# Token projection in three rounded products over two neighbouring banks, and weights' transposes that wait only for what they read

## The chip, the core and the metric

The kernel runs on one core of a Trainium2 chip. The metric is the device time of one execution in microseconds (us). Before the change three runs took 1888.12 to 1890.75, median 1889.14.

## The reference

One transformer layer on 2048 tokens of width 512: latent attention with 16 heads, then a feed-forward matrix, each with a residual and a layer norm. All is float32. The part that the change touches is the projection of the tokens at the head of the attention:

```python
cq = rms_norm(hidden_states @ w_qa.T, q_a_ln_w)          # 384 columns
ckv = hidden_states @ w_kva.T                            # 128 + 64 columns
k_pe = ckv[..., KVLR:].reshape(b, s, 1, DR).transpose(0, 2, 1, 3)
k_pe = k_pe * cos + rotate_half(k_pe) * sin
ckv_l = rms_norm(ckv[..., :KVLR], kv_a_ln_w)
```

So each token is multiplied by 576 columns of weights. `cq` later makes the queries; `ckv_l` is key and value of every head (the heads' own matrices are folded into the queries' and the output's weights by the kernel); `k_pe` is the rotary part of the keys.

## The kernel before

The program has three phases, each a block of its own in which all engines start together: preparing (lines 96 to 578), attention, and the output's feed-forward. Only the first is touched. It runs a hardware loop of four iterations `c`; each treats four tiles `t` of 128 tokens and, beside them, one group of four heads' weights.

A tile goes like this. TensorE turns its x with four transposes into bank X (`turn_x`, line 331); ScalarE copies it to `x_t` (`copy_x`, line 443). TensorE multiplies it by the turned weights `wa_t` (`project`, lines 343 and 351): a plain float32 product counts two matmul records per 128 rows, so a tile has 8 records of 512 columns into bank `PROJ` and 8 of the last 64 columns into `KP`. ScalarE takes the sums of squares of the 384 and the 128 columns (474, 476). VectorE makes the rotary part (545 to 551) and adds the epsilon (555), POOL raises to the power -1/2 (284). ScalarE scales the 384 columns to `cq_n` (482), VectorE the 128 to `c_n` (561), and makes the value tiles (567, 569). TensorE transposes the results (`turn_results`, lines 359 to 366). Then each result is stored in two rounded (fp32r) halves: `hi` on ScalarE rounds it (467, 469), `lo` on VectorE stores the remainder (530, 532); `tok_lo` counts the remainders, three a tile.

Beside tile t TensorE does some of the 14 fills of the heads' weights (`beside`: fills 0 to 2, 3 to 6, 7 to 9, 10 and 11; 12 and 13 at the end): three products of 512 columns ("nope", line 385), three pairs of transposes ("pe", 391), four times four transposes ("turn", 397) and four products ("out", 404). ScalarE and VectorE empty each by `split` as rounded value and remainder (458, 522), a "turn" by one copy (450). The fills use banks 5 to 7 in turn.

The order on every engine is that of the code. TensorE: `project(t)`, `turn_x(t+1)`, the fills beside t, `turn_results(t-1)`. ScalarE: squares, copy of the next x, splits, `cq_n(t)`, `hi(t-1)`. VectorE: rotary part, epsilon, splits, `c_n(t)`, `lo(t-1)`. After the loop the angles' tables are transposed, copied and stored to DRAM by 16 DMAs of SP; then the attention starts.

At the start SP issues the loads one after the other: identity, w_qa, w_kva, its tail, both norms' weights, mask, cos, sin, and a copy of x to DRAM; POOL issues x and the first group's weights. TensorE waits for identity, both norms and all of w_qa and w_kva, then turns them (316, 318); ScalarE copies them (436, 437).

Of the kernel before, what the change touches and what calls it, by code (L numbers as in the profile page):

```python
# [14 lines left out]
P = 128  # L15
S = 2048
HID = 512
# [21 lines left out]
def chunk(c):  # L39

    return (c + 1) % NCH
# [54 lines left out]
def prepare_phase(nc, m, x, w_qa, w_kva, w_qb, w_kvb, w_o, q_ln, kv_ln, ident_in, mask_in, cos_in, sin_in):  # L96
# [6 lines left out]
    with ExitStack() as ctx:  # L103
# [10 lines left out]
        def sb(name, n):  # L114
            return ctx.enter_context(nc.sbuf_tensor(name, [P, n], F32))[:, :]
# [8 lines left out]
        wa_t = stage(KH * WA).rearrange("p (k n) -> p k n", k=KH)  # L124
        x_in = stage(4 * HID).rearrange("p (t i) -> p t i", t=4)
        x_t = [sb(f"x_t{b}", HID) for b in range(2)]
# [18 lines left out]
        const_loaded = sem("const_loaded")  # L145
        consts_made = sem("consts_made")
        wa_loaded = sem("wa_loaded")
        wa_turned = sem("wa_turned")
        wa_copied = sem("wa_copied")
# [3 lines left out]
        xt_copied = sem("xt_copied")  # L153
# [30 lines left out]
        X, PROJ, TR = m.bank[0], m.bank[1:3], m.bank[3]  # L184
        KP, KT = m.bank[4][:, 0:DR], m.bank[4][:, P:2 * P]
# [24 lines left out]
        def fill_bank(n):  # L210
            return m.bank[5 + n % 3]

        def last_in_bank(n):

            return max(f for f in range(FILLS) if f % 3 == n % 3)
# [19 lines left out]
        def _(sp):  # L235
            sp.dma_start(m.ident[:, :], ident_in).then_inc(const_loaded, 16)
            sp.dma_start(wa_rows[:, 0:3, :], w_qa.rearrange("(o p) i -> p o i", p=P)).then_inc(wa_loaded, 16)
            sp.dma_start(wa_rows[:, 3, :], w_kva[0:C]).then_inc(wa_loaded, 16)
            sp.dma_start(wa_tail[0:DR], w_kva[C:C + DR]).then_inc(wa_loaded, 16)
            sp.dma_start(q_w, q_ln.rearrange("(k p) -> p k", p=P),  # L240
                         allow_slow_non_contiguous=True).then_inc(const_loaded, 16)
            sp.dma_start(kv_w, kv_ln.rearrange("(k p) -> p k", p=P),
                         allow_slow_non_contiguous=True).then_inc(const_loaded, 16)
# [66 lines left out]
        def _(pe):  # L310
            pe.wait_ge(const_loaded, 16 * 3)
            pe.wait_ge(wa_loaded, 48)

            for k in range(KH):
                for o in range(4):
                    pe.transpose(m.bank[k][:, o * P:o * P + P], wa_rows[:, o, k * P:k * P + P], m.ident[:, :])
            for k in range(KH):
                mm = pe.transpose(m.bank[4][:, k * DR:k * DR + DR], wa_tail[0:DR, k * P:k * P + P],
                                  m.ident[0:DR, 0:DR])
            mm.then_inc(wa_turned, 1)  # L320
            pe.wait_ge(wa_copied, KH + 1)
# [96 lines left out]
            pe.wait_ge(xt_copied, NCH * 4 + 1)  # L418
# [7 lines left out]
        def token_places(c, t):  # L426
# [3 lines left out]
            yield KT, lambda a: m.key_pe[:, a, bass.ds(chunk(c) * 512 + t * P, P)], None  # L430

        @block.scalar
        def _(act):
            act.wait_ge(wa_turned, 1)
            for k in range(KH):
                nc.scalar.copy(wa_t[:, k, 0:QLR + C], m.bank[k]).then_inc(wa_copied, 1)
            nc.scalar.copy(wa_t[:, :, QLR + C:WA], m.bank[4][:, 0:KH * DR].rearrange("p (k n) -> p k n", k=KH)
                           ).then_inc(wa_copied, 1)
            act.wait_ge(consts_made, 4)

            def copy_x(c, t):
                act.wait_ge(x_turned, 1 if c is None else c * 4 + t + 1)
                nc.scalar.copy(x_t[t % 2], X).then_inc(xt_copied, 1)

            copy_x(None, 0)
            with act.Fori(0, NCH) as c:
# [24 lines left out]
                for t in range(4):  # L471
                    b = t % 2
                    act.wait_ge(proj_ready, c * 4 + t + 1)
                    nc.scalar.activation(squares[:, 0:QLR], PROJ[b][:, 0:QLR], ACT.Square, scale=QLR ** -0.5,
                                         accum_out=means[:, 2 * b:2 * b + 1]).then_inc(squared, 1)
                    nc.scalar.activation(squares[:, QLR:QLR + C], PROJ[b][:, QLR:QLR + C], ACT.Square, scale=C ** -0.5,
                                         accum_out=means[:, 2 * b + 1:2 * b + 2]).then_inc(squared, 1)
                    copy_x(c, t + 1)
# [3 lines left out]
                    nc.scalar.activation(cq_n[b], PROJ[b][:, 0:QLR], ACT.Copy,  # L482
# [21 lines left out]
        def _(dve):  # L504
            nc.vector.memset(minus_half, -0.5).then_inc(consts_made, 1)
            dve.wait_ge(const_loaded, 16 * 3)
            nc.vector.tensor_copy(m.ident16[:, :], m.ident[:, :]).then_inc(consts_made, 1)
            dve.wait_ge(wq_free, 16)
            nc.vector.tensor_copy(m.mask16[:, :], mask).then_inc(consts_made, 1)

            nc.vector.tensor_scalar(q_w, q_w, SCALE, None, ALU.mult).then_inc(consts_made, 1)
            dve.wait_ge(consts_made, 4)
            dve.wait_ge(wo_free, 16)
            dve.wait_ge(cq_free, 16)
            nc.vector.memset(m.small[:, 60:61], 0.0).then_inc(tok_lo, TOK)
            nc.vector.memset(m.small[:, 61:62], 0.0).then_inc(split_lo, SPLITS)
            with dve.Fori(0, NCH) as c:
# [17 lines left out]
                for t in range(4):  # L535
# [4 lines left out]
                    kp = KP.rearrange("p (a d) -> p a d", a=2)  # L540
# [20 lines left out]
                    nc.vector.tensor_scalar(c_n[b], PROJ[b][:, QLR:QLR + C], rstd[:, 2 * b + 1:2 * b + 2],  # L561
# [1188 lines left out]
```

## Time and profile before

| what | us |
|---|---|
| median of three runs | 1889.14 |
| profiled execution | 1888.2 |
| its span (first to last instruction) | 1886.5 |
| before the loop | 0 to 24.3 |
| four iterations | 24.3 to 156.3 |
| table copies and stores | to 176.4 |
| attention and feed-forward | from 176.4 |

Over the span TensorE (PE) is busy 91%, VectorE (DVE) 74%, ScalarE (ACT) 58%, GpSimd (POOL) 52%. In the views PE is a matmul or transpose, PEld the load of its stationary operand. A line of a timeline joins neighbouring instructions of one kind (x8 is eight), with the start of the first; the duration of the last runs on while the next instruction begins, so the pace of matmuls is read from one start to the next. A bracket says how long the engine was idle before it and what ended that. PEclk is the granted clock of TensorE, 1.00 for 2.4 GHz and 0.50 for 1.2 GHz.

### The profile page before, as it was taken

What the parts mean: (1) busy time and instruction counts of PE and PEld (TensorE: products, weight loads), DVE (VectorE), ACT (ScalarE), POOL (GpSimd) and SP (SyncE); (2) the same over time, 40 slices, a digit from 0 to 9 for tenths busy, and PEclk for the clock granted to TensorE, in tenths of its full rate; (3) what the DMA queues carried; (4) which work ended last, traced back from release to release, by engine and by line L of the source; (5) the groups of instructions that cost most, each with busy time, mean ns of one, the idle gap of its engine ahead of it and who ended that gap; (6) DMA issues with size and microseconds to landing.
All of it is one profiled execution on the core that took longest, in us unless ns stands there. A gap on an engine that the chain in (4) does not pass through costs nothing. (4 is left out here: it accounts for less than half of the span.)

```text
span 1886.5 us, 28030 instructions
## 1 busy us (share of the span) xinstructions
PE 1725.7 (91%) x8729; PEld 1396.3 (74%) x8729; DVE 1393.6 (74%) x2503; ACT 1096.9 (58%) x2092; POOL 971.9 (52%) x883
## 2 busy tenths in 40 slices
PE   5995699999999999999988899999999999998586
PEld 4564578888888888888877688888887887886442
DVE  1552368888888888878766588888888888888366
ACT  2553256666676666657545566666666766666220
POOL 2320135555555555556543455565555665556455
PEclk9997899999999999999989899999999999999889
DMA  7876212121211311112121221212112111100321
GB/s 231 305 304 211 64 49 62 46 68 40 92 50 57 98 60 52 61 51 84 57 67 34 94 75 36 67 39 96 49 53 101 42 48 35 52 31 31 123 73 56
DMA packets 90138, 152.99 MB, mean 81 GB/s; under 512 B 17872, under 2 KB 60368, under 8 KB 87632
## 3 DMA queue, kind: packets, MB, share of 16 engines
q1 hardware_dynamic: 81168, 103.60, 17.5%
q0 software_dynamic: 7104, 23.60, 3.8%
q10 hardware_dynamic: 1728, 24.12, 3.0%
q8 instruction: 67, 1.10, 0.2%
q14 instruction: 71, 0.58, 0.1%
HBM read 87.30 MB, written 51.38 MB: 74 GB/s over the span
## 5 line engine op out<-in xcount | busy, mean ns | idle before, releaser
L1320 POOL TENSOR_TENSOR split_p<-pool,split_p 128x512 fp32r<-128x512 f32 x544 | 702.9, 1294 | 542.3 <-ACT split_p L1265 541.9
L1143 PE MATMUL rows<-q_c,key_c 128*128 128x512 f32 x1632 | 478.9, 402 | 27.9 <-issue 15.9
L1253 ACT COPY pool<-rows 128x512 f32<-128x512 f32 x480 | 281.8, 587 | 266.7 <-PE rows L1143 264.7
L1397 DVE TENSOR_TENSOR top<-rows,top 128x512 f32<-128x512 f32 x420 | 289.0, 688 | 146.6 <-ACT pool L1253 143.5
L1412 DVE TENSOR_TENSOR pool<-bank,pool 128x512 f32<-128x512 f32 x544 | 370.1, 680 | 27.0 <-PE bank L1161 27.0
L1258 ACT ACTIVATE pool<-pool 128x512 f32<-128x512 f32 x544 | 345.9, 636 | 18.8 <-DVE pool L1412 18.3
L1265 ACT CAST split_p<-pool 128x512 fp32r<-128x512 f32 x544 | 333.2, 612 | 25.0 <-PE bank L1174 25.0
L1143 PEld LDWEIGHTS rows<-q_c,key_c 128*128 128x128 f32 x1632 | 290.4, 190 | 76.2 <-issue 27.1
L1143 PE MATMUL rows<-q_pe,key_pe 128*128 128x512 f32 x1088 | 339.1, 393 | 0.0
L1424 DVE TENSOR_TENSOR bank<-bank,pool 128x512 f32<-128x512 f32 x480 | 331.1, 690 | 0.1
L1143 PEld LDWEIGHTS rows<-q_pe,key_pe 128*128 128x128 f32 x1088 | 205.7, 189 | 45.6
L1171 PE MATMUL bank<-split_p,val 128*128 128x512 f32 x544 | 215.1, 395 | 9.2 <-ACT o_sum L1271 9.0
L1174 PE MATMUL bank<-split_p,val 128*128 128x512 f32 x544 | 214.8, 395 | 5.2 <-POOL split_p L1320 4.9
L1172 PE MATMUL bank<-split_p,val 128*128 128x512 f32 x544 | 213.2, 392 | 0.0
L1203 PE MATMUL rows<-wo,o_t 128*128 128x512 f32 x528 | 136.2, 408 | 22.9 <-POOL o_t L1325 18.3
L1203 PEld LDWEIGHTS rows<-wo,o_t 128*128 128x128 f32 x528 | 101.1, 196 | 55.7 <-issue 34.3
L1325 POOL TENSOR_TENSOR o_t<-o_sum,o_t 128x512 fp32r<-128x512 f32 x64 | 82.4, 1287 | 94.9 <-ACT o_t L1283 94.7
L1171 PEld LDWEIGHTS bank<-split_p,val 128*128 128x128 f32 x544 | 102.5, 188 | 34.8 <-ACT o_sum L1271 11.7
L1174 PEld LDWEIGHTS bank<-split_p,val 128*128 128x128 f32 x544 | 102.7, 189 | 33.2 <-POOL split_p L1320 11.5
L1172 PEld LDWEIGHTS bank<-split_p,val 128*128 128x128 f32 x544 | 102.7, 189 | 21.3
L1283 ACT CAST o_t<-o_sum 128x512 fp32r<-128x512 f32 x64 | 39.7, 620 | 126.2 <-DVE o_sum L1436 99.0
L1109 PE MATMUL rows<-cq,wq 128*128 128x256 f32 x792 | 105.0, 287 | 0.0
(159 smaller groups left out, 2058.8 us busy)
## 6 DMA issues: line engine op xcount, KB each, us to landing
cq<-cq_dram SPq DMA_DIRECT2D x28, 768.0 KB, 5.0
y<-y_dram SPq DMA_DIRECT2D x64, 256.0 KB, 3.0
y_dram<-y SPq DMA_DIRECT2D x64, 256.0 KB, 2.0
wq_dram<-wq ACTq DMA_DIRECT2D x4, 2304.0 KB, 11.5
wo_dram<-wo ACTq DMA_DIRECT2D x4, 2048.0 KB, 10.6
q_pe<-by_sin SPq DMA_DIRECT2D x256, 32.0 KB, 1.8
q_pe<-by_cos SPq DMA_DIRECT2D x256, 32.0 KB, 1.8
table<-table_dram SPq DMA_DIRECT2D x31, 256.0 KB, 2.9
```

What stands on the lines that cost most here:

```text
L1143: mm = pe.matmul(by_head(out), k, q, start=(z == 0), stop=(z == 4))
L1171: pe.matmul(OUT, m.val[:, 0, j, :], split_p[:, n % 2, 0, :], start=(t == 0), stop=False)
L1172: pe.matmul(OUT, m.val[:, 1, j, :], split_p[:, n % 2, 0, :], start=False, stop=False)
L1174: pe.matmul(OUT, m.val[:, 0, j, :], split_p[:, n % 2, 1, :], start=False, stop=(t == keys(it) - 1)).then_inc(values_done, 1)
L1203: mm = pe.matmul(aux(u), o_t[:, a, h * P:h * P + P], m.wo[:, b, h, :], start=(n == 0), stop=(n == 3 * HG - 1))
L1253: nc.scalar.copy(slot(n), SCORES[n % N_SCORES]).then_inc(scores_copied, 1)
L1258: nc.scalar.activation(slot(n), slot(n), ACT.Exp).then_inc(exp_done, 1)
L1265: nc.scalar.copy(split_p[:, n % 2, 0, :], slot(n)).then_inc(p_hi, 1)
L1320: nc.gpsimd.tensor_tensor(split_p[:, n % 2, 1, :], slot(n), stored(split_p[:, n % 2, 0, :]), ALU.subtract).then_inc(p_lo, 1)
L1397: nc.vector.tensor_tensor(out, SCORES[n % N_SCORES], slot(number(it, 0)) if t == 1 else out, ALU.max).then_inc(scores_maxed, 1)
L1412: nc.vector.tensor_tensor(slot(n), MAXES, slot(n), ALU.add).then_inc(shifted, 1)
L1424: nc.vector.tensor_tensor(TOTAL, TOTAL, slot(n), ALU.add).then_inc(summed, 1)
```

## The change

- x and the turned weights are each kept as a rounded value and a rounded remainder (`x_hi`, `x_lo`, `wa_hi`, `wa_lo`). ScalarE's copy makes the first, a new subtraction on VectorE the second (`rest_of_x`, one per tile, and five for the weights). The projection is hi by hi, hi by lo and lo by hi: 3 x 4 stationary operands, each against two halves of 288 columns, 24 matmuls a tile.
- The 576 columns lie across the border of two neighbouring banks, in bank pairs 0, 1 and 2, 3 by turns. The turned rotary part of tile t lies in the same pair as its products. x is turned in bank 4, results in bank 5, and fills have banks 6 and 7.
- `project(t)` waits for the remainders (`tok_lo`) of the tile two before ahead of its first matmul.
- ScalarE copies the next x before the squares, and waits for the rotary parts ahead of the squares.
- Weights' transposes wait for the identity and w_qa and w_kva alone, and the tail's for the tail. w_kva is loaded ahead of w_qa. The angles come in quarters, the first iteration's ahead of the norms' weights, the others behind the mask; they are waited for in the loop. VectorE's first memset of `tok_lo`, which the first projection now waits for, stands behind the mask, the norms' weights and the first quarter.

```diff
-        X, PROJ, TR = m.bank[0], m.bank[1:3], m.bank[3]
-        KP, KT = m.bank[4][:, 0:DR], m.bank[4][:, P:2 * P]
+        X, TR, PART = m.bank[4], m.bank[5], WA // 2
+
+        def projected(t):
+
+            return m.rows[:, 1024 * (t % 2) + 512 - PART:1024 * (t % 2) + 512 + PART]
+
+        def turned_rotary(t):
+
+            return m.rows[:, 1024 * (t % 2) + 1024 - P:1024 * (t % 2) + 1024]
...
         def fill_bank(n):
-            return m.bank[5 + n % 3]
+            return m.bank[6 + n % 2]
...
-            sp.dma_start(m.ident[:, :], ident_in).then_inc(const_loaded, 16)
+            def load_angles(c):
+                for table, source in ((cos, cos_in), (sin, sin_in)):
+                    sp.dma_start(table[:, 4 * chunk(c):4 * chunk(c) + 4, :],
+                                 source.rearrange("(t p) d -> p t d", p=P)[:, 4 * chunk(c):4 * chunk(c) + 4, :]
+                                 ).then_inc(angles_loaded[c > 0], 16)
+
+            sp.dma_start(m.ident[:, :], ident_in).then_inc(ident_loaded, 16)
+            sp.dma_start(wa_rows[:, 3, :], w_kva[0:C]).then_inc(wa_loaded, 16)
             sp.dma_start(wa_rows[:, 0:3, :], w_qa.rearrange("(o p) i -> p o i", p=P)).then_inc(wa_loaded, 16)
-            sp.dma_start(wa_rows[:, 3, :], w_kva[0:C]).then_inc(wa_loaded, 16)
-            sp.dma_start(wa_tail[0:DR], w_kva[C:C + DR]).then_inc(wa_loaded, 16)
+            sp.dma_start(wa_tail[0:DR], w_kva[C:C + DR]).then_inc(tail_loaded, 16)
+            load_angles(0)
...
             sp.dma_start(mask, mask_in).then_inc(wq_free, 16)
-            sp.dma_start(cos, cos_in.rearrange("(t p) d -> p t d", p=P)).then_inc(wo_free, 16)
-            sp.dma_start(sin, sin_in.rearrange("(t p) d -> p t d", p=P)).then_inc(cq_free, 16)
+            for c in range(1, NCH):
+                load_angles(c)
 
...
-            pe.wait_ge(const_loaded, 16 * 3)
-            pe.wait_ge(wa_loaded, 48)
+            pe.wait_ge(ident_loaded, 16)
+            pe.wait_ge(wa_loaded, 32)
 
             for k in range(KH):
                 for o in range(4):
-                    pe.transpose(m.bank[k][:, o * P:o * P + P], wa_rows[:, o, k * P:k * P + P], m.ident[:, :])
+                    mm = pe.transpose(m.bank[k][:, o * P:o * P + P], wa_rows[:, o, k * P:k * P + P], m.ident[:, :])
+                mm.then_inc(wa_turned, 1)
+            pe.wait_ge(tail_loaded, 16)
             for k in range(KH):
-                mm = pe.transpose(m.bank[4][:, k * DR:k * DR + DR], wa_tail[0:DR, k * P:k * P + P],
+                mm = pe.transpose(TR[:, k * DR:k * DR + DR], wa_tail[0:DR, k * P:k * P + P],
                                   m.ident[0:DR, 0:DR])
             mm.then_inc(wa_turned, 1)
-            pe.wait_ge(wa_copied, KH + 1)
...
-                    pe.wait_ge(xt_copied, c * 4 + t)
+                    pe.wait_ge(x_rest, c * 4 + t)
...
             turn_x(None, 0)
+            pe.wait_ge(wa_rest, 1)
             with pe.Fori(0, NCH) as c:
 
                 def project(t):
-                    pe.wait_ge(xt_copied, c * 4 + t + 1)
+                    pe.wait_ge(x_rounded, c * 4 + t + 1)
                     if t >= 2:
 
-                        pe.wait_ge(cn_done, c * 4 + t - 1)
-                    for k in range(KH):
-                        pe.matmul(PROJ[t % 2], x_t[t % 2][:, k * P:k * P + P], wa_t[:, k, 0:QLR + C],
-                                  start=(k == 0), stop=(k == KH - 1))
-
-
-                    if t:
-                        pe.wait_ge(rope_parts, c * 12 + 3 * t)
-                    pe.wait_ge(tok_lo, TOK + c * TOK + 3 * max(t - 1, 0))
-                    for k in range(KH):
-                        mm = pe.matmul(KP, x_t[t % 2][:, k * P:k * P + P], wa_t[:, k, QLR + C:WA],
-                                       start=(k == 0), stop=(k == KH - 1))
+                        pe.wait_ge(tok_lo, TOK + c * TOK + 3 * (t - 1))
+                    else:
+                        pe.wait_ge(tok_lo, c * TOK + 3 * (t + 3))
+                    terms = [(x_hi, wa_hi, k) for k in range(KH)] + [(x_hi, wa_lo, k) for k in range(KH)] \
+                        + [(x_lo, wa_hi, k) for k in range(KH)]
+                    for n, (xs, ws, k) in enumerate(terms):
+                        if n == 2 * KH:
+                            pe.wait_ge(x_rest, c * 4 + t + 1)
+                        for at in (0, PART):
+                            mm = pe.matmul(projected(t)[:, at:at + PART], xs[t % 2][:, k * P:k * P + P],
+                                           ws[:, k, at:at + PART], start=(n == 0), stop=(n == 3 * KH - 1))
                     mm.then_inc(proj_ready, 1)
 
...
                     pe.wait_ge(krot_done, c * 8 + 2 * t + 2)
-                    if t < 3:
-
-                        pe.wait_ge(rope_parts, c * 12 + 3 * t + 6)
-                    pe.transpose(KT, k_rot[t % 2], m.ident[:, :]).then_inc(turned, 1)
+                    pe.transpose(turned_rotary(t), k_rot[t % 2], m.ident[:, :]).then_inc(turned, 1)
...
-                    if n < 3:
+                    if n < 2:
                         pe.wait_ge(split_lo, c * SPLITS + split_of[last_in_bank(n)] + 1)
                     else:
-                        if fills[n - 3][0] == "turn":
-                            pe.wait_ge(wot_copied, c * HG + fills[n - 3][1] + 1)
+                        if fills[n - 2][0] == "turn":
+                            pe.wait_ge(wot_copied, c * HG + fills[n - 2][1] + 1)
                         else:
-                            pe.wait_ge(split_lo, SPLITS + c * SPLITS + split_of[n - 3] + 1)
+                            pe.wait_ge(split_lo, SPLITS + c * SPLITS + split_of[n - 2] + 1)
...
-            act.wait_ge(wa_turned, 1)
...
+                act.wait_ge(wa_turned, k + 1)
+                nc.scalar.copy(wa_hi[:, k, 0:QLR + C], m.bank[k]).then_inc(wa_rounded, 1)
...
             copy_x(None, 0)
+            act.wait_ge(consts_made, 4)
...
                     act.wait_ge(proj_ready, c * 4 + t + 1)
-                    nc.scalar.activation(squares[:, 0:QLR], PROJ[b][:, 0:QLR], ACT.Square, scale=QLR ** -0.5,
+                    copy_x(c, t + 1)
+                    act.wait_ge(rope_parts, c * 12 + 3 * t + 3)
+                    nc.scalar.activation(squares[:, 0:QLR], projected(b)[:, 0:QLR], ACT.Square, scale=QLR ** -0.5,
                                          accum_out=means[:, 2 * b:2 * b + 1]).then_inc(squared, 1)
-                    nc.scalar.activation(squares[:, QLR:QLR + C], PROJ[b][:, QLR:QLR + C], ACT.Square, scale=C ** -0.5,
+                    nc.scalar.activation(squares[:, QLR:QLR + C], projected(b)[:, QLR:QLR + C], ACT.Square, scale=C ** -0.5,
                                          accum_out=means[:, 2 * b + 1:2 * b + 2]).then_inc(squared, 1)
-                    copy_x(c, t + 1)
                     for n in beside[t]:
...
+            def rest_of_x(c, t):
+                dve.wait_ge(x_rounded, 1 if c is None else c * 4 + t + 1)
+                nc.vector.tensor_tensor(x_lo[t % 2], X, stored(x_hi[t % 2]), ALU.subtract).then_inc(x_rest, 1)
+
...
-            dve.wait_ge(const_loaded, 16 * 3)
+            dve.wait_ge(ident_loaded, 16)
             nc.vector.tensor_copy(m.ident16[:, :], m.ident[:, :]).then_inc(consts_made, 1)
+            for k in range(KH):
+                dve.wait_ge(wa_rounded, k + 1)
+                nc.vector.tensor_tensor(wa_lo[:, k, 0:QLR + C], m.bank[k], stored(wa_hi[:, k, 0:QLR + C]), ALU.subtract)
+            dve.wait_ge(wa_rounded, KH + 1)
+            nc.vector.tensor_tensor(wa_lo[:, :, QLR + C:WA], wa_tails(), stored(wa_hi[:, :, QLR + C:WA]), ALU.subtract
+                                    ).then_inc(wa_rest, 1)
+            rest_of_x(None, 0)
             dve.wait_ge(wq_free, 16)
             nc.vector.tensor_copy(m.mask16[:, :], mask).then_inc(consts_made, 1)
 
+            dve.wait_ge(wo_free, 16)
+            dve.wait_ge(cq_free, 16)
             nc.vector.tensor_scalar(q_w, q_w, SCALE, None, ALU.mult).then_inc(consts_made, 1)
             dve.wait_ge(consts_made, 4)
-            dve.wait_ge(wo_free, 16)
-            dve.wait_ge(cq_free, 16)
+            dve.wait_ge(angles_loaded[0], 32)
             nc.vector.memset(m.small[:, 60:61], 0.0).then_inc(tok_lo, TOK)
             nc.vector.memset(m.small[:, 61:62], 0.0).then_inc(split_lo, SPLITS)
...
-                    kp = KP.rearrange("p (a d) -> p a d", a=2)
+                    if t == 3:
+                        dve.wait_ge(angles_loaded[1], 32 * (NCH - 1))
+                    kp = projected(t)[:, QLR + C:WA].rearrange("p (a d) -> p a d", a=2)
...
+                    rest_of_x(c, t + 1)
...
```

The copy of the weights on ScalarE goes bank by bank, each followed by VectorE's subtraction.

## Rows read from the trace of the kernel before

**Rows 1.** Second iteration: us, busy of PE, PEld, DVE, ACT, POOL, PEclk, DMA share.

```profile
58.48:91.09 32.61, 30.11 (x156) 19.76 (x155) 16.84 (x59) 18.29 (x50) 10.33 (x17) 1.00 0.79 301
```

**Rows 2.** Timeline of TensorE in that iteration: start, us, engine, line, operation, idle before.

```profile
58.48 3.69 PE L343 MATMUL rows<-pool,x_t 128*128 128x512 f32 x8
...
63.29 2.84 PE L385 MATMUL bank<-pool 128*128 128x128 f32 x24
65.97 3.60 PE L343 MATMUL rows<-pool,x_t 128*128 128x512 f32 x8
...
70.24 0.61 PE L331 MATMUL rows<-ident,pool 128*128 128x128 f32 x4
...
72.71 0.66 PE L397 MATMUL bank<-ident,pool 128*128 128x128 f32 x4 [1.20 <-DVE wq L522]
...
73.75 3.60 PE L343 MATMUL rows<-pool,x_t 128*128 128x512 f32 x8
...
90.49 0.55 PE L359 MATMUL rows<-ident,cq_n 128*128 128x128 f32 x3 [1.30 <-DVE key_pe L530]
```

**Rows 3.** Timeline of ScalarE and VectorE, the iteration's second tile.

```profile
70.44 0.49 ACT L474 ACTIVATE squares<-rows 128x384 f32<-128x384 f32 x1 [3.11 <-PE bank L351]
...
71.17 0.59 ACT L443 COPY x_t<-rows 128x512 f32<-128x512 f32 x1
...
73.89 0.59 ACT L482 ACTIVATE cq_n<-rows,small 128x384 f32<-128x384 f32 x1
...
74.50 0.35 DVE L561 TENSOR_SCALAR c_n<-rows,small 128x128 f32<-128x128 f32 x1 [1.07 <-ACT cq_n L482]
...
76.30 0.28 DVE L530 TENSOR_TENSOR key_pe<-bank,key_pe 128x128 f32 x1
```

**Rows 4.** Timeline of TensorE in the attention: rounded (fp32r) matmuls at full clock.

```profile
183.11 2.32 PE L1109 MATMUL bank<-cq,wq 128*128 128x256 f32 x18
185.27 1.00 PE L1122 MATMUL rows<-cq,wq 128*128 128x256 f32 x7
...
205.97 0.86 PE L1143 MATMUL rows<-q_c,key_c 128*128 128x512 f32 x3
206.67 0.63 PE L1143 MATMUL rows<-q_pe,key_pe 128*128 128x512 f32 x2
```

**Rows 5.** Groups of instructions by line, the span's first 180 us: busy us, mean ns.

```profile
L522 DVE SCALAR_TENSOR_TENSOR wq<-bank,small,wq 128x512 fp32r<-128x512 f32 x12 | 9.0, 751 | 5.1 <-ACT wq L458 4.2
...
L458 ACT ACTIVATE wq<-bank,small 128x512 fp32r<-128x512 f32 x12 | 8.2, 687 | 1.7 <-PE bank L385 0.8
...
L522 DVE SCALAR_TENSOR_TENSOR wq<-bank,small,wq 128x256 fp32r<-128x256 f32 x12 | 5.1, 478 | 2.7 <-ACT wq L458 2.7
...
L458 ACT ACTIVATE wq<-bank,small 128x256 fp32r<-128x256 f32 x12 | 4.9, 498 | 0.0
```

**Rows 6.** Line 1369, attention: ns min/median/max, first and last start us.

```profile
L1369 DVE TENSOR_TENSOR q_c<-bank,q_c x20: 682/691/693, 186.1 to 1703.9; 128x512 fp32r<-128x512 f32 x20
```

**Rows 7.** Timeline of TensorE at the loop's start and in the attention, and one stage.

```profile
24.30 5.13 PE L343 MATMUL rows<-pool,x_t 128*128 128x512 f32 x8 [0.74 <-ACT x_t L443]
...
1039.72 0.50 PE L1171 MATMUL bank<-split_p,val 128*128 128x512 f32 x1 [2.77 <-ACT o_sum L1271]
...
1041.10:1044.50 3.40, 3.40 (x10) 2.63 (x9) 3.27 (x6) 2.87 (x6) 3.40 (x4) 0.52 0.00 0
```

**Rows 8.** Timeline of the start, and a DMA issue (KB, us from issue to landing).

```profile
1.78 0.49 SPq L238 DMA_DIRECT2D wa_rows<-in_L_attn_w_kva  x1
...
16.19 3.67 PE L316 MATMUL rows<-ident,wa_rows 128*128 128x128 f32 x16 [16.19 <-DMA small<-in_L_attn_kv_a_ln_w]
...
17.64 0.23 DVE L509 CAST mask<-pool 128x128 bf16<-128x128 f32 x1 [1.25 <-DMA pool<-const_mask]
...
22.26 0.06 DVE L515 MEMSET small<- 128x1 f32 x1 [4.31 <-DMA sin<-const_sin]
...
wa_rows<-in_L_attn_w_kva SPq DMA_DIRECT2D x1, 256.0 KB, 7.0
```

More of the change, by code:

```diff
@@ L112, in stage, with sb @@
             return m.pool[:, at - n:at]
-        def sb(name, n):
-            return ctx.enter_context(nc.sbuf_tensor(name, [P, n], F32))[:, :]
+        def sb(name, n, dt=F32):
+            return ctx.enter_context(nc.sbuf_tensor(name, [P, n], dt))[:, :]
         WA = QLR + C + DR
@@ L123, in prepare_phase @@
         mask = stage(P)
-        wa_t = stage(KH * WA).rearrange("p (k n) -> p k n", k=KH)
         x_in = stage(4 * HID).rearrange("p (t i) -> p t i", t=4)
-        x_t = [sb(f"x_t{b}", HID) for b in range(2)]
+        wa_hi = sb("wa_hi", KH * WA, F32R).rearrange("p (k n) -> p k n", k=KH)
+        wa_lo = sb("wa_lo", KH * WA, F32R).rearrange("p (k n) -> p k n", k=KH)
+        x_hi = [sb(f"x_hi{b}", HID, F32R) for b in range(2)]
+        x_lo = [sb(f"x_lo{b}", HID, F32R) for b in range(2)]
         cq_n = [sb(f"cq_n{b}", QLR) for b in range(2)]
@@ L143, in prepare_phase @@
         rstd = m.small[:, 16:20]
-        const_loaded = sem("const_loaded")
+        ident_loaded = sem("ident_loaded")
+        angles_loaded = [sem(f"angles_loaded{n}") for n in range(2)]
         consts_made = sem("consts_made")
         wa_loaded = sem("wa_loaded")
+        tail_loaded = sem("tail_loaded")
         wa_turned = sem("wa_turned")
-        wa_copied = sem("wa_copied")
+        wa_rounded = sem("wa_rounded")
+        wa_rest = sem("wa_rest")
         x_loaded = [sem(f"x_loaded{t}") for t in range(4)]
         x_turned = sem("x_turned")
-        xt_copied = sem("xt_copied")
+        x_rounded = sem("x_rounded")
+        x_rest = sem("x_rest")
         proj_ready = sem("proj_ready")
@@ L180, in prepare_phase, with wa_tails @@
         wo_free, cq_free = m.wo_free, m.cq_free
-        X, PROJ, TR = m.bank[0], m.bank[1:3], m.bank[3]
-        KP, KT = m.bank[4][:, 0:DR], m.bank[4][:, P:2 * P]
+        X, TR, PART = m.bank[4], m.bank[5], WA // 2
[3 more added lines that the diff above has]
+            return m.rows[:, 1024 * (t % 2) + 1024 - P:1024 * (t % 2) + 1024]
+        def wa_tails():
+            return TR[:, 0:KH * DR].rearrange("p (k n) -> p k n", k=KH)
         fills = [("nope", k) for k in range(KR)] + [("pe", k) for k in range(KR)] \
@@ L210, in fill_bank @@
         def fill_bank(n):
-            return m.bank[5 + n % 3]
+            return m.bank[6 + n % 2]
         def last_in_bank(n):
-            return max(f for f in range(FILLS) if f % 3 == n % 3)
+            return max(f for f in range(FILLS) if f % 2 == n % 2)
         def split_places(n):
@@ L235, in _ @@
         def _(sp):
[L236 removed]
+            def load_angles(c):
[5 more added lines that the diff above has]
+            sp.dma_start(wa_rows[:, 3, :], w_kva[0:C]).then_inc(wa_loaded, 16)
             sp.dma_start(wa_rows[:, 0:3, :], w_qa.rearrange("(o p) i -> p o i", p=P)).then_inc(wa_loaded, 16)
[L238 to L239 removed]
+            sp.dma_start(wa_tail[0:DR], w_kva[C:C + DR]).then_inc(tail_loaded, 16)
+            load_angles(0)
             sp.dma_start(q_w, q_ln.rearrange("(k p) -> p k", p=P),
[L241 removed]
+                         allow_slow_non_contiguous=True).then_inc(wo_free, 16)
             sp.dma_start(kv_w, kv_ln.rearrange("(k p) -> p k", p=P),
[L243 removed]
+                         allow_slow_non_contiguous=True).then_inc(cq_free, 16)
             sp.dma_start(mask, mask_in).then_inc(wq_free, 16)
[L245 to L246 removed]
+            for c in range(1, NCH):
+                load_angles(c)
             sp.dma_start(m.y_dram.rearrange("t p d -> (t p) d"), x).then_inc(m.y_stored, 16)
@@ L417, in _ @@
             pe.wait_ge(split_lo, SPLITS * (NCH + 1))
-            pe.wait_ge(xt_copied, NCH * 4 + 1)
+            pe.wait_ge(x_rest, NCH * 4 + 1)
             for w, source in enumerate((cos, sin)):
@@ L429, in token_places @@
             yield TR[:, QLR:QLR + C], lambda a: m.key_c[:, a, bass.ds(chunk(c) * 512 + t * P, P)], kv_w
-            yield KT, lambda a: m.key_pe[:, a, bass.ds(chunk(c) * 512 + t * P, P)], None
+            yield turned_rotary(t), lambda a: m.key_pe[:, a, bass.ds(chunk(c) * 512 + t * P, P)], None
         @block.scalar
         def _(act):
-            act.wait_ge(wa_turned, 1)
             for k in range(KH):
[L436 to L439, printed above, removed]
+                act.wait_ge(wa_turned, k + 1)
+                nc.scalar.copy(wa_hi[:, k, 0:QLR + C], m.bank[k]).then_inc(wa_rounded, 1)
+            act.wait_ge(wa_turned, KH + 1)
+            nc.scalar.copy(wa_hi[:, :, QLR + C:WA], wa_tails()).then_inc(wa_rounded, 1)
             def copy_x(c, t):
                 act.wait_ge(x_turned, 1 if c is None else c * 4 + t + 1)
-                nc.scalar.copy(x_t[t % 2], X).then_inc(xt_copied, 1)
+                nc.scalar.copy(x_hi[t % 2], X).then_inc(x_rounded, 1)
             copy_x(None, 0)
+            act.wait_ge(consts_made, 4)
             with act.Fori(0, NCH) as c:
@@ L481, in _ @@
                     act.wait_ge(rstd_done, c * 4 + t + 1)
-                    nc.scalar.activation(cq_n[b], PROJ[b][:, 0:QLR], ACT.Copy,
+                    nc.scalar.activation(cq_n[b], projected(b)[:, 0:QLR], ACT.Copy,
                                          scale=rstd[:, 2 * b:2 * b + 1]).then_inc(cqn_done, 1)
@@ L560, in _ @@
                     dve.wait_ge(cqn_done, c * 4 + t + 1)
-                    nc.vector.tensor_scalar(c_n[b], PROJ[b][:, QLR:QLR + C], rstd[:, 2 * b + 1:2 * b + 2],
+                    nc.vector.tensor_scalar(c_n[b], projected(b)[:, QLR:QLR + C], rstd[:, 2 * b + 1:2 * b + 2],
                                             None, ALU.mult).then_inc(cn_done, 1)
```

## The prediction

> **What bounds the kernel now.** I read the stages first: one of the four iterations of the preparing loop takes 32.61 us, TensorE works in 30.11 of them at clock 1.00 [rows 1]. The reader is to see that this stage, unlike the attention behind it, is one that the diff touches, and that TensorE has 2.5 us of idle time in an iteration. Next, TensorE's timeline of that iteration [rows 2]: a tile's projection starts at 65.97 and the transposes of the next x at 70.24, so it takes 4.27 us. The idle time lies in two places, 1.20 us ahead of line 397 and 1.30 us ahead of line 359, and both end with a remainder of VectorE. Last, ScalarE's and VectorE's timeline of the same tile [rows 3]: the last remainder of tile 0's results (`lo(0)`, line 530, key_pe) ends at 76.30 + 0.28 = 76.58, which is 2.83 us after the projection of tile 2 began (73.75). That lateness costs little today, since only the 64-column product waits for it, behind 3.4 us of the 512-column one.
>
> **The projection.** Removed: 16 matmuls a tile in 4.27 us. Added: 24 rounded ones of 288 columns. The nearest rows are the rounded matmuls of the attention [rows 4]: 18 of 256 columns from 183.11 to 185.27, 0.120 us each; three of 512 from 205.97 to 206.67, 0.233 each. On the line between them 288 columns are 0.134, and 24 are 3.20 us. The ends are 2.88 and 5.6; I take 3.20 because 288 is near 256. Saved: 1.07 us a tile, 17 us in all, if TensorE alone set the pace. The Trainium skill ("TensorE: Matmul & The Clock Gate", "Back-to-back issue gap") gives a sustained spacing of about 131 ns at 512 columns, by which this projection would be an estimated 2.4 us (a rival, below); the trace shows 233 ns there [rows 4], so this case does not bear it out.
>
> **The new wait.** `project(t)` for t = 2 and 3 now waits for `lo(t-2)` ahead of its first matmul, because rotary transposes and products share banks. `lo(t-2)` stands on VectorE behind `c_n(t-1)`, that behind ScalarE's `cq_n(t-1)`, and that behind the projection of t-1. So projections 1, 2, 3 and the end of the iteration become one chain through three engines. I walk one iteration from the start of projection 0, with the intervals of rows 2, 3, 5 and 6. ScalarE starts 0.20 us after TensorE's last matmul (70.24 to 70.44) [rows 2, 3]; squares take 0.73 (to 71.17), `cq_n` to `c_n` 0.61, `c_n` to the end of `lo` 2.08 (74.50 to 76.58) [rows 3]. A 512-wide eviction is 0.69 on ScalarE and 0.75 on VectorE, a 256-wide one 0.50 and 0.48 [rows 5]. The new rounding's remainder of x on VectorE is like line 1369, 0.69 [rows 6]; it lies beside ScalarE's squares and sets nothing. The same holds for ScalarE's new wait for the rotary parts, done by 3.96 us where the copy of x ends at 4.44.
> - Step 0: projection to 3.20, x turned at 3.65, copied from 3.85, squares 4.33 to 5.06, first eviction 5.75, its remainder 6.55. Two fill banks instead of three let the third fill start only then (6.6, not 5.44); with 0.89 for it (24 matmuls, three fills, from 63.29 to 65.97 [rows 2]) tile 1 starts at 7.5. Before: 7.49. The third bank's loss eats the whole gain.
> - Step 1: projection to 10.7, x turned at 11.15, two small fills to 11.6. The third and fourth wait for remainders in their banks, 13.7 and 14.1; transposed results of tile 0 end at 15.1. ScalarE: squares 11.85, evictions, the copy of fill 6 at 14.7, `cq_n` 15.2; VectorE `c_n` 15.8, `lo(0)` done 17.9. Projection 2 starts at 17.95, after 2.9 us of idle TensorE. Step: 10.45 us, against 7.78 [rows 2].
> - Step 2: projection to 21.15, x turned at 21.6, the third turned fill waits for its bank (23.7), last copy 24.3, `cq_n` 24.8, `c_n` 25.4, `lo(1)` 27.5. Projection 3 at 27.55, again after 2.9 us of idling.
> - Step 3: projection to 30.75, two output fills to 32.9, `cq_n` 33.85, `c_n` 34.7, `lo(2)` 36.8, results of tile 3 turned in 0.55 to 0.60 [rows 2]: 37.4.
>
> So an iteration is 37.4 us, not 32.61: +4.8, four times +19.2. Today `lo(0)` ends 10.61 us after projection 1 began [rows 2, 3], 0.2 more than my walk has; with as much in three steps, and as much again for hand-overs I overlooked, 1.2 us an iteration is the upper bound, +5. The lower is 24 matmuls at 0.120, 0.32 us in each of four steps, -5.
>
> **The clock.** TensorE will be idle about 2.1 and 2.9 us around a few transposes in step 1, and 1.2 and 2.9 in step 2; today's loop has nothing over 1.3. In the attention an idle of 2.77 us was followed by a stretch at 0.52 [rows 7]. Eight 512-column matmuls took 5.13 us at the start, where the clock had fallen, and 3.60 later [rows 2, 7]: 1.53 a fall. Ends: no fall, and eight (two an iteration) of 1.7. I take eight of 1.3, since some of a slow stretch lies in idle time: +10.4. The fall at the first projection stays as it is.
>
> **The start.** Weights' transposes began at 16.19 on the landing of kv_ln, though w_kva, the last that most of them read, landed at 1.78 + 7.0 = 8.8 [rows 8]. All of their work, with 4 copies, 4 remainders (0.6 and 0.7 apiece) and x's first rounding, fits between 9 and 15. But projection 0 now also waits for VectorE's memset behind mask, both norms and the first quarter of the angles. Today that memset is at 22.26, behind the whole tables [rows 8], and projection 0 at 24.30, behind the transposes [rows 7]. SP issues the small loads later (two quarter tables ahead of them, 1024 packets of 128 B), with 3072 packets of the other quarters moved behind; POOL's weight loads run beside them as now, and one x load is issued as soon as the first x is turned. Mask today lands at 17.6, sin at 22.2 [rows 8]. Between these, and 1 us on either side, 18.5 to 23 for the memset: I take projection 0 at 21.5, -2.8. Moved behind as well are the copy of x to y, and the six other quarters that SP issues. Tile 3 alone waits for those quarters, some 25 us later, and the copy is read only in the attention. Where the cover of the early weights goes, nothing is lost: they end 6 us ahead of need.
>
> **Sum** against the profiled execution's own 1888.2 us (its span is 1886.5; 0.9 under the median 1889.14 of the runs): -2.8 + 19.2 + 10.4 = +26.8, **1915 us**. Attention and the feed-forward behind it start as soon as the stage ends and are unchanged, the table's stores after the loop included.
>
> **Rivals.**
> - The same wait, clock unhurt: 1888.2 - 2.8 + 19.2 = 1904.6. For it: 1.3 us of idling does nothing today, and transposes break the gaps. Against it: [rows 7].
> - Faster: TensorE's work sets the loop and the remainders come in time. The place is the wait at projections 2 and 3; it decides if `lo(0)` ends before tile 0's results are turned, so 2.8 us sooner than now. Then each of 16 tiles saves 1.07 and the start 2.8: 1868. Against it stands 76.58 over 73.75 [rows 2, 3], and that each link of the chain follows from the one before.
> - Products of 288 columns cost like 512 ones: 24 x 0.233 = 5.6 us, +2.4 on each of 16 tiles on top of the forecast, 1953. Rows at 256 speak against it.
> - Products cheaper than any row here, at 0.100 us apiece: 0.8 less on each of 16 tiles, 1902. No row goes below 0.120 for 256 columns [rows 4]. This is where the Trainium skill's spacing ("TensorE: Matmul & The Clock Gate", "Back-to-back issue gap") would put it.
> - The change does not remove the start's wait (other loads land late as well): +2.8, 1918. The order of the queue speaks against it; it is inside the range.
> - The clock stays low for most of the stage: an iteration's four projections, 12.8 us on the chain, double, +51 in all on the unhurt clock's time: 1956.
>
> **How the numbers follow.** Forecast 0.60 (the late start within it), unhurt clock 0.23, cheaper products 0.03, low clock or dear products together 0.06, faster 0.04, and 0.04 that start and walk are so far off that they cancel. The range goes from the unhurt clock less the cheaper matmuls (1900) to eight full falls and today's latencies (some 1925, with 1 for the start): 1900 to 1926. A measurement of this kernel tells about 0.2% (3.8 us) from nothing. Faster 0.04, same 0.04, slower 0.92.
>
> **What would show it.** Right: an iteration of 37 to 41 us; PE's first matmul of projections 2 and 3 idle about 2.9 us until DVE key_pe; fill 2 waiting for a remainder of wq; clock under 1.00 inside the loop; projections of 3.2 us at full clock; projection 0 near 21.5. Wrong: idle under 1 us ahead of projections 2 and 3, an iteration under 33, or rounded matmuls off 0.134 by more than 0.02.

## The result, and the profile after

The changed kernel took 1925.75 us (median of four runs, 1923.99 to 1926.6), the kernel before 1889.95 beside it: a ratio of 1.0182, 95% interval 1.0166 to 1.0197. It is slower by 36 us. I had said 1915, in a range of 1900 to 1926; the direction and the place were right, the size was 10 us short, and the time lies only 0.25 us under the range's upper end.

The four steps of the second iteration, from the start of one tile's projection to the next (stages view of the changed kernel: length, then busy us of PE, PEld, DVE, ACT, POOL, then the granted clock, DMA share, GB/s):

```profile
66.50:74.08 7.58, 6.58 (x54) 6.39 (x53) 4.61 (x13) 3.39 (x10) 1.82 (x4) 1.00 1.04 414
74.08:84.70 10.62, 5.89 (x46) 5.22 (x44) 6.32 (x20) 5.56 (x15) 2.00 (x3) 0.88 0.58 222
84.70:96.33 11.63, 7.87 (x45) 7.40 (x45) 3.44 (x13) 4.16 (x12) 3.94 (x7) 0.79 0.16 31
96.33:107.79 11.46, 10.18 (x46) 7.40 (x47) 5.65 (x17) 5.13 (x13) 2.52 (x4) 0.87 0.92 361
```

The sum is 41.29 us, against 32.61 in [rows 1]. The reader is to see two things: the first step is as long as before (7.58 against 7.49), and the clock, 1.00 in every iteration before but the first, is 0.79 to 0.88 in the other three steps. TensorE's timeline of the same iteration shows why:

```profile
66.50 1.32 PE L376 MATMUL rows<-wa_hi,x_hi 128*128 128x288 f32 x8
...
69.78 0.60 PE L356 MATMUL bank<-ident,pool 128*128 128x128 f32 x4
70.22 1.95 PE L407 MATMUL bank<-pool 128*128 128x128 f32 x16
73.16 1.16 PE L407 MATMUL bank<-pool 128*128 128x128 f32 x8 [0.99 <-DVE wq L557]
74.08 1.30 PE L376 MATMUL rows<-wa_hi,x_hi 128*128 128x288 f32 x8
...
77.34 0.60 PE L356 MATMUL bank<-ident,pool 128*128 128x128 f32 x4
...
80.24 0.44 PE L413 MATMUL bank<-ident,pool 128*128 128x128 f32 x2 [1.87 <-DVE wq L557]
...
84.70 2.29 PE L376 MATMUL rows<-wa_hi,x_hi 128*128 128x288 f32 x8 [2.86 <-DVE key_pe L565]
...
89.90 0.60 PE L356 MATMUL bank<-ident,pool 128*128 128x128 f32 x4
...
96.33 2.29 PE L376 MATMUL rows<-wa_hi,x_hi 128*128 128x288 f32 x8 [2.74 <-DVE key_pe L565]
...
100.91 0.60 PE L356 MATMUL bank<-ident,pool 128*128 128x128 f32 x4
...
107.79 1.31 PE L376 MATMUL rows<-wa_hi,x_hi 128*128 128x288 f32 x8
```

A projection at full clock takes 74.08 to 77.34, 3.26 us for 24 matmuls. Ahead of projections 2 and 3 TensorE stands idle 2.86 and 2.74 us until the last remainder of the tile two before, and these two projections then take 5.20 and 4.58 us. VectorE's side of the first of these waits, from the same kernel's timeline, answers to [rows 3]:

```profile
82.43 0.35 DVE L599 TENSOR_SCALAR c_n<-rows,small 128x128 f32<-128x128 f32 x1 [0.72 <-ACT cq_n L505]
...
84.37 0.28 DVE L565 TENSOR_TENSOR key_pe<-rows,key_pe 128x128 f32 x1
```

`lo(0)` ends at 84.65 (84.37 + 0.28), 10.57 us after projection 1 began; before it was 10.61. The chain has kept its length, and the projection that once ran beside its last part now runs behind it.

The start, from the timeline of all engines, answers to [rows 8]:

```profile
6.03 4.05 SPq L266 DMA_DIRECT2D small<-in_L_attn_kv_a_ln_w  x1
...
8.55 3.65 PE L340 MATMUL rows<-ident,wa_rows 128*128 128x128 f32 x16 [8.55 <-DMA wa_rows<-in_L_attn_w_qa]
...
10.12 0.86 SPq L268 DMA_DIRECT2D pool<-const_mask  x1
...
21.69 0.23 DVE L543 CAST mask<-pool 128x128 bf16<-128x128 f32 x1 [6.48 <-DMA pool<-const_mask]
...
22.11 0.06 DVE L550 MEMSET small<- 128x1 f32 x1
...
22.23 2.29 PE L376 MATMUL rows<-wa_hi,x_hi 128*128 128x288 f32 x8 [8.37 <-DVE small L550]
```

The weights' transposes start 7.6 us earlier, and TensorE then waits 8.37 us for the memset, which stands behind the mask's cast. The mask was issued at 10.12 (4.13 before) and landed at 21.6. The first projection is 2.07 us earlier than before.

Where the 38.4 us between the two spans lie: -2.1 at the start, +38.3 in the loop (22.23 to 192.49, 170.26 us, against 132.0), -0.2 in the tables, and +2.4 in the attention and the feed-forward, whose code is the same.

### The profile page after: what moved, and what is told of

Read it like the earlier page. It is cut to its first block and busy times, and to the rows that moved or that the text cites. A ratio compares the mean times of both kernels' runs of the same rounds, so it can differ in the third digit from the quotient of the medians.

```text
span 1924.9 us, 28312 instructions
## 1 busy us (share of the span) xinstructions
PE 1733.2 (90%) x8857; PEld 1430.5 (74%) x8857; DVE 1408.8 (73%) x2525; ACT 1097.6 (57%) x2092; POOL 972.8 (51%) x883
```

## The experiments

### The wait alone, in the kernel before

```diff
                         pe.wait_ge(cn_done, c * 4 + t - 1)
+                        pe.wait_ge(tok_lo, TOK + c * TOK + 3 * (t - 1))
                     for k in range(KH):
                         pe.matmul(PROJ[t % 2], x_t[t % 2][:, k * P:k * P + P], wa_t[:, k, 0:QLR + C],
```

> The kernel before with one wait more: the projections of tiles 2 and 3 wait for the remainders of the tile two before ahead of their first matmul. If that wait and the clock behind it are the loss, TensorE stands idle 2.8 us ahead of projection 2 and 3.3 ahead of projection 3 in each iteration (+22 us in four, some 2 given back by the product that waited before), and a fallen clock adds 1.5 to 2 us to each of these eight projections: +32 to +38, some 1920 to 1927. If the loss lies in the rounded products, their remainders or the banks, this costs nothing of note: within 3 us of before.

Measured: 1939.22 us against 1894.19 of the kernel before on that chip, a ratio of 1.0234 (1.0208 to 1.0259): +45. One iteration and its two waits, in the stages view and TensorE's timeline of this kernel:

```profile
70.72:115.06 44.34, 35.92 (x157) 21.92 (x155) 16.87 (x59) 18.22 (x50) 10.37 (x17) 0.85 0.61 224
```

```profile
88.88 6.02 PE L344 MATMUL rows<-pool,x_t 128*128 128x512 f32 x8 [2.73 <-DVE key_pe L531]
94.74 1.00 PE L352 MATMUL bank<-pool,x_t 128*128 128x64 f32 x8
...
101.22 6.67 PE L344 MATMUL rows<-pool,x_t 128*128 128x512 f32 x8 [3.18 <-DVE key_pe L531]
107.73 1.00 PE L352 MATMUL bank<-pool,x_t 128*128 128x64 f32 x8
```

With no rounded product, no second remainder and three fill banks, an iteration is 11.7 us longer than 32.61: 5.9 of idling and 5.5 in which the two 512-column products take 5.86 and 6.51 us (88.88 to 94.74, 101.22 to 107.73) in place of 3.43. This wait makes such a loss by itself, and more than the +32 to +38 that I expected: I had priced a fall of the clock at 1.5 to 2 us a projection, and it is 2.4 and 3.1. Over the eight projections 2 and 3 of the profile it is 23.7 us of idling and 21.5 of slower products, together the 45.

### TensorE kept busy while it waits

```diff
                     if t >= 2:
+                        pe.wait_ge(x_rest, c * 4 + t + 1)
+                        for _ in range(12):
+                            pe.matmul(X, wa_hi[:, 0, 0:P], wa_hi[:, 0, 0:512], start=True, stop=True)
                         pe.wait_ge(tok_lo, TOK + c * TOK + 3 * (t - 1))
```

> The changed kernel with 12 idle matmuls of 512 columns (about 2.8 us at full clock) into the bank of the turned x, while projections 2 and 3 wait. They compute nothing that is used. If the slow projections are a matter of the clock, the 15.4 us by which projections 2 and 3 exceed 3.27 us vanish and the iteration falls to 38 us: some 1910 to 1913. If they are slow for another reason (two engines reading beside them, operands), the projections keep 4.6 to 5.9 us and the time stays at 1926 or rises by the overhang of the idle matmuls.

Measured: 1910.80 us against 1894.19, a ratio of 1.0089 (1.0071 to 1.0107). The changed kernel itself, run later on one chip with the kernel before, had 1925.27 against 1892.18, 1.0177 (1.0160 to 1.0194). Its expectation:

> The changed kernel unaltered, on the chip of the runs beside it: +36 to +37 us over before, as in the first measurement.

It was 33 over there, a little under the 36 expected. So the added work takes the loss from 33 to 36 us down to 17 (13 to 20 by the interval), within the 1910 to 1913 expected. The four steps again, in the stages view of the kernel kept busy:

```profile
62.82:70.40 7.58, 6.59 (x54) 6.40 (x53) 4.61 (x13) 3.38 (x10) 1.82 (x4) 1.00 1.03 386
70.40:81.02 10.62, 8.66 (x59) 7.37 (x57) 6.33 (x20) 5.55 (x15) 2.00 (x3) 1.00 0.68 264
81.02:90.73 9.71, 8.69 (x57) 7.62 (x57) 3.43 (x13) 4.15 (x12) 3.95 (x7) 1.00 0.20 31
90.73:100.74 10.01, 8.82 (x48) 6.11 (x47) 5.49 (x17) 5.12 (x13) 2.48 (x4) 1.00 1.01 402
```

The clock is 1.00, and the sum is 37.92. All projections of the kernel behind the first take 3.2 to 3.3 us; in the last iteration the clock still fell once, ahead of the added matmuls, which took 4.4 us in place of 3.0. My walk had said 7.5, 10.45, 9.6 and 9.85. This is the walk's own case, the wait without the clock, and it parts the loss: the projections were slow for the clock, not for their operands or for what ran beside them, since both are the same here.

### Two fill banks, in the kernel before

```diff
         def fill_bank(n):
-            return m.bank[5 + n % 3]
+            return m.bank[5 + n % 2]
```

(and `n - 3`, `n < 3` and `n % 3` in the waits likewise)

> The kernel before with two fill banks instead of three and nothing else. If the third bank's loss is a cost of its own, fills 2, 6, 9 and 12 wait 0.3 to 0.7 us each: up to 1.7 us an iteration, +4 to +7. If the waits for remainders at the end of each tile hide it, within 2 us of before.

Measured: 1901.91 against 1894.19, 1.0038 (1.0023 to 1.0052). The expectation's upper end was +7; it is +7.7 between the medians, so I had it a little too cheap. TensorE's timeline shows the waits:

```profile
61.04 3.69 PE L343 MATMUL rows<-pool,x_t 128*128 128x512 f32 x8
...
68.56 1.16 PE L385 MATMUL bank<-pool 128*128 128x128 f32 x8 [0.75 <-DVE wq L522]
...
76.30 0.44 PE L391 MATMUL bank<-ident,pool 128*128 128x128 f32 x2 [1.43 <-DVE wq L522]
...
84.06 0.66 PE L397 MATMUL bank<-ident,pool 128*128 128x128 f32 x4 [0.58 <-ACT pool L450]
...
95.86 3.68 PE L343 MATMUL rows<-pool,x_t 128*128 128x512 f32 x8
```

An iteration is 34.82 us, 2.2 more than with three banks, where I had allowed 1.7. So the third bank is worth over half of what the cheaper products can save (1.0 us on each of four tiles).

### The wait moved behind a projection

```diff
         def turned_rotary(t):
-            return m.rows[:, 1024 * (t % 2) + 1024 - P:1024 * (t % 2) + 1024]
+            return X[:, 0:P]
...
                     pe.wait_ge(x_rest, c * 4 + t)
+                    pe.wait_ge(tok_lo, TOK + c * TOK + 3 * max(t - 2, 0))
...
                     if t >= 2:
-                        pe.wait_ge(tok_lo, TOK + c * TOK + 3 * (t - 1))
-                    else:
-                        pe.wait_ge(tok_lo, c * TOK + 3 * (t + 3))
+                        pe.wait_ge(cn_done, c * 4 + t - 1)
...
                     pe.wait_ge(krot_done, c * 8 + 2 * t + 2)
+                    pe.wait_ge(x_rest, c * 4 + min(t + 3, 5))
```

> The changed kernel with the turned rotary part in the bank of the turned x, so that projections wait only for their own products to be read, and the wait for the remainders stands ahead of the next turning of x, behind a projection. If the early wait was the loss, iterations fall to 31 to 32 us with the clock at 1.00, and the start gains some 5 us: 1878 to 1884. If the three products, the new remainders or the two fill banks cost the time, iterations stay over 36 and the time over 1900.

Measured: 1884.14 against 1894.19, 0.9950 (0.9933 to 0.9966). All of the change but the place of one 128-column transpose, and the waits that go with it, is in here, and it is 10 us faster than before instead of 36 slower (1884.14 is just over the expected 1878 to 1884). The second iteration in the stages view, and its waits in TensorE's timeline:

```profile
51.93:83.77 31.84, 26.77 (x188) 23.19 (x187) 19.89 (x63) 18.31 (x50) 10.27 (x17) 1.00 0.82 313
```

```profile
58.59 1.16 PE L407 MATMUL bank<-pool 128*128 128x128 f32 x8 [0.99 <-DVE wq L557]
...
65.67 0.44 PE L413 MATMUL bank<-ident,pool 128*128 128x128 f32 x2 [1.86 <-DVE wq L557]
...
72.79 0.66 PE L419 MATMUL bank<-ident,pool 128*128 128x128 f32 x4 [1.02 <-ACT pool L472]
...
83.07 0.55 PE L383 MATMUL bank<-ident,cq_n 128*128 128x128 f32 x3 [0.68 <-DVE key_pe L565]
```

TensorE works 3.3 us less in this iteration than before, but waits 5.1 instead of 2.5, mostly for the two fill banks. The clock is 1.00 here, but not to the end. In the third iteration the same wait of 1.86 us is followed by slow transposes and a slow first part of projection 2:

```profile
97.50 0.44 PE L413 MATMUL bank<-ident,pool 128*128 128x128 f32 x2 [1.86 <-DVE wq L557]
...
99.56 2.20 PE L375 MATMUL rows<-wa_hi,x_hi 128*128 128x288 f32 x8
101.59 1.23 PE L375 MATMUL rows<-wa_lo,x_hi 128*128 128x288 f32 x8
```

That iteration takes 33.41 us (83.77 to 117.18) at a mean clock of 0.95, and in the fourth projection 2 takes 4.80. Where the gain lies is told by two starts of projection 1 in the first iteration, before and here:

```profile
33.23 3.60 PE L343 MATMUL rows<-pool,x_t 128*128 128x512 f32 x8
```

```profile
27.46 1.30 PE L375 MATMUL rows<-wa_hi,x_hi 128*128 128x288 f32 x8
```

It is 5.8 us earlier here, because projection 0 no longer waits for the memset, and the attention's first instruction is 6.0 us earlier (170.43 against 176.38). So in the profile the whole gain is made at the start, and the rest of the loop, from projection 1 on, is as long as before: what the cheaper products save, some 0.8 us an iteration, two falls of the clock take back.

### The start alone, in the kernel before

The loads, semaphores and waits of the changed kernel as in its diff; projection, banks and engines' orders of before.

> The kernel before with the changed loads and the changed waits of the weights' transposes alone. In the changed kernel the start gained 2.1 us, because projection 0 waited for VectorE's memset at 22.1. Here only the 64-column product waits for it: if that wait was what held the gain back, the first tile is projected around 23.0 instead of 30.1 and the whole gains 5 to 7 us. If the small loads themselves hold it back, it gains under 2.

Measured: 1884.58 against 1892.18, 0.9958 (0.9941 to 0.9976), that is 7.6 us, or 4.5 to 11; its seven runs spread over 10 us. TensorE's timeline:

```profile
15.17 6.15 PE L354 MATMUL rows<-pool,x_t 128*128 128x512 f32 x8 [0.68 <-ACT x_t L454]
21.84 1.10 PE L362 MATMUL bank<-pool,x_t 128*128 128x64 f32 x8 [0.52 <-DVE small L528]
22.78 0.61 PE L342 MATMUL rows<-ident,pool 128*128 128x128 f32 x4
```

The wide product is done before the memset comes, at half the pace (6.15 us for what takes 3.6 later) and at no cost; x is turned at 22.78, against 30.11 before. The part of the change that I gave 2.8 us is worth 7.6 where only the narrow product waits. In the changed kernel, whose whole first projection waits for the memset, x is turned at 27.89: the wait took most of the gain back. And this kernel, with the old products and three banks, is as fast as the one with the moved wait, within the intervals.

### Work put into the waits for banks

```diff
-                    for n in beside[t]:
+                    early = 2
+                    for n in beside[t][:early]:
                         fill(n)
                     if t:
                         turn_results(t - 1)
+                    for n in beside[t][early:]:
+                        fill(n)
```

in the kernel with the wait moved.

> rotary_in_x with the transposes of a tile's results ahead of the last fills of its step, so that they fill the waits of 1.9 and 1.0 us for the two fill banks. If TensorE's waits for banks now set the loop, an iteration falls by 0.5 to 1.1 us from 31.8: 2 to 4 us less than rotary_in_x, 12 to 14 under before. If the chain of ScalarE and VectorE sets it, no change.

Measured: 1878.79 against 1892.18, 0.9935 (0.9918 to 0.9951), the lowest of all, though its interval overlaps those of the other three fast kernels. The 13.4 us under before are the 12 to 14 expected, but not for the reason expected. The iteration from 50.47 to 81.97 is 31.50, only 0.34 less, where I expected 0.5 to 1.1. Another 1.2 us lie at the start, where projection 1 begins at 26.26 instead of 27.46; the edit changes nothing there, and what differs is the pace: the 24 matmuls of the first fills took 4.47 us in the kernel before this edit and go at full pace here. The largest part lies in the third and fourth iterations: the clock stays at 1.00 in them (32.65 us from 81.97 to 114.62, against 33.41). That the broken-up wait keeps the clock up fits this and is not tested apart. In the first iteration:

```profile
31.52 0.33 PE L388 MATMUL bank<-ident,k_rot 128*128 128x128 f32 x1 [0.53 <-DVE x_lo L533]
32.42 0.44 PE L413 MATMUL bank<-ident,pool 128*128 128x128 f32 x2 [0.57 <-DVE wq L560]
...
37.16 0.66 PE L357 MATMUL bank<-ident,pool 128*128 128x128 f32 x4 [0.51 <-DVE key_pe L568]
```

The wait of 1.9 us has become two of about half a microsecond, the first of them for the new remainder of x, and a third has come ahead of the turning of x, so the loop may now run close to the chain of the other engines; no run shows that by itself.

### The memsets first

```diff
             nc.vector.memset(minus_half, -0.5).then_inc(consts_made, 1)
+            nc.vector.memset(m.small[:, 60:61], 0.0).then_inc(tok_lo, TOK)
+            nc.vector.memset(m.small[:, 61:62], 0.0).then_inc(split_lo, SPLITS)
```

in the kernel of the experiment ahead, where they stood behind the mask, the norms' weights and the first quarter of the angles.

> results_between with VectorE's two memsets ahead of all its waits. The second turning of x then starts near 17.4 instead of 22.1, and ScalarE is held until 22 by the norms' weights: 2 us less than results_between. If the start is bound by TensorE's fills at half clock and the memset is hidden, no change.

Measured: 1881.21 against 1892.18, 0.9944 (0.9928 to 0.9961): 2.4 us more than the kernel without it, where I had expected 2 less, and the two intervals overlap. TensorE's timeline:

```profile
18.48 1.95 PE L407 MATMUL bank<-pool 128*128 128x128 f32 x16
25.04 2.08 PE L407 MATMUL bank<-pool 128*128 128x128 f32 x8 [4.60 <-DVE wq L560]
26.77 2.27 PE L375 MATMUL rows<-wa_hi,x_hi 128*128 128x288 f32 x8
...
31.92 0.60 PE L357 MATMUL bank<-ident,pool 128*128 128x128 f32 x4
```

Two fills come 4 us earlier, the third then waits 4.60 us, and then takes 1.73 us (25.04 to 26.77), and the next projection 5.15 (26.77 to 31.92); the kernel without the edit had 0.91 and 3.26 there. What came earlier only made TensorE wait longer, and the lower clock behind the wait (0.50 from 25.04 to 26.77) made it dearer. The remainder that the third fill waits for stands on VectorE behind the mask's cast, at 21.60 there.

## Why the prediction was right, and what was off

- **The wait** (+19.2 forecast). Right, and shown twice: alone it makes the kernel before 45 us slower, and moved behind a projection it turns 36 us of loss into 10 of gain, some 6 of which are the start's. Idle 2.9 us was forecast ahead of both projections; 2.74 to 3.15 stands in the profile of the changed kernel, but once 2.32. The walk of 7.5, 10.45, 9.6 and 9.85 met 7.58, 10.62, 9.71 and 10.01 in the kernel kept busy. It was 0.5 short an iteration, 2 us in all, within the bound of 5.
- **The clock** (+10.4 forecast). This is the term that was mis-sized. The eight projections 2 and 3 took 41.55 us where eight at full clock take 26.2: +15.4 (41.4 in the kernel's second profile). I had taken 1.3 a fall, out of the 1.53 of the first projection of before [rows 7], and 1.7 as its upper end. It was 1.3 to 2.65, 1.9 in the mean. From 24.30 on, before, the half clock lasted 3 us of the projection; here, low from before the projection's start, it lasted 2.6 to 5.3 us of it. The step at fault is that one fall's price was read from a single row and called typical, and then lowered because some of a slow stretch lies in idle time, though that row itself stands behind an idle and holds only what is left after it. The first projection, which I left as it was, also lost 2.4 where it lost 1.5 before.
- **The start** (-2.8 forecast, -2.1 measured). The gate was the one named, the memset behind the small loads. It came at 22.11; SP was held 4.05 us by the issue of kv_ln, 0.53 before, and issued the mask only at 10.12. Another order of the small loads was not tried.
- **The products** (0.134 us apiece, 3.20 a tile). 24 in 3.26, 0.136. The line between the rows of 256 and 512 columns [rows 4] was good, and the dearer and the cheaper rival both fall. The Trainium skill ("TensorE: Matmul & The Clock Gate", "Back-to-back issue gap") has 131 ns at 512 columns, and this case's trace has 233 [rows 4].
- **The two fill banks.** Right for step 0, where they eat the gain whole (from 5.44 to 6.6 us into the step in the walk, so 1.2 of wait, and 0.99 measured).
- Not foreseen is what has no code in the diff: attention and feed-forward took 2.4 us more in the first profile.
- **The range** held by a hair, and by luck. Its upper end had eight falls at 1.7 us, +13.6, and the clock took 15.4; what kept the time inside is that the walk was 2 us short where 5 were allowed.

The faster rival, "the remainders come in time", is what the moved wait made true, and it gives 0.5%, not its 1868: I had left the two banks out of its price, and falls of the clock that their longer wait (1.86 us for 1.20) still brings. The rival without a clock, 1904.6, is the kernel kept busy, 17 us over before. That this is so near the forecast +16.4 is partly luck: in the profiles its attention starts 21.5 us later than before, from a loop 23.5 us longer and a start 2.0 shorter. Of the 23.5 the walk had 19.2; the rest is its 2 us, 0.8 more at the first projection, and the one fall.

## What to carry to other kernels

When a change shares a bank between two things, ask what is released last and put the wait for it behind work that does not need it: here the place of one small transpose decided between 36 us lost and 10 won. A wait on TensorE cost its idle time and then a slower stretch of seven to nine tenths of that (15.4 us behind 22.1 of idling in the changed kernel, 21.5 behind 23.7 with the wait alone), so price both, the second from several falls in the trace. And a matmul saving is worth no more than what buffers, the other engines' chain and the clock let through: 1.0 us a tile on paper came out as 0.8 us in four tiles of the second iteration, and as nothing over the whole loop. One iteration at full clock does not stand for all four.

## What the runs showed that was not expected

- Around each idle of 2.3 to 3.3 us ahead of a projection the granted clock was low, in both kernels that have such waits, and all of those projections were slow; with the idle filled by work without use, none was. The slow stretch outlasted the idle: in step 2 of the changed kernel the mean clock is 0.79 over 11.6 us, and 0.59 over the projection itself (84.70 to 89.90).
- The length of an idle alone did not decide. The wait of 1.86 us in step 1 left the clock at 1.00 in two iterations of the kernel with the moved wait and was followed by slow matmuls in the other two.
- PEclk can be wrong in the first microseconds: it reads 1.00 from 15.17 to 21.32 in the kernel with the start alone, where the matmuls go at half the pace.
- The same phases of attention and feed-forward, in unchanged code, took from 1710 to 1716 us between profiles (1924.9 less 212.36 in the changed kernel's; 1925.7 less 210.35 in its second), so differences of 2 or 3 us between kernels that end their first stage at different times are not settled by one profile. The first instruction of the attention parts the two. The kernel before was profiled once, beside the first runs only, so up to 5 us of the differences below have no place in a profile:

| kernel | attention starts at, us | less 176.4 | median less before's |
|---|---|---|---|
| changed | 212.4 | +36.0 | +35.8 |
| changed, again | 210.4 | +34.0 | +33.1 |
| the wait alone | 223.9 | +47.5 | +45.0 |
| kept busy | 197.9 | +21.5 | +16.6 |
| two fill banks | 185.4 | +9.0 | +7.7 |
| wait moved | 170.4 | -6.0 | -10.1 |
| start alone | 169.0 | -7.4 | -7.6 |
| results between | 166.0 | -10.4 | -13.4 |
| memsets first | 168.2 | -8.2 | -11.0 |

- The issue of a small load on SP is not a constant: kv_ln's took 4.05 us with a quarter of the tables ahead of it, and 0.53 before. In the kernel before it is the issue of sin, behind the whole of cos, that held SP, for 13.20 us.
